# Causal attention: one exponential over all four heads of a step

## What is computed

```python
def _attn(x, ln_w, ln_b, conv_w, attn_w, proj_w, n_head):
    ...
    q = q * cos + _rotate_half(q) * sin
    k = k * cos + _rotate_half(k) * sin
    scores = jnp.einsum('bqhd,bkhd->bhqk', q, k) / jnp.sqrt(jnp.float32(D))
    causal = jnp.tril(jnp.ones((T, T), dtype=bool))
    scores = jnp.where(causal, scores, jnp.float32(-1e+30))
    p = jax.nn.softmax(scores, axis=-1)
    y = jnp.einsum('bhqk,bkhd->bqhd', p, v).reshape(B, T, C)
    return y @ proj_w
```

## Time and profile before

| | |
|---|---|
| median of 3 runs | 433.37 us (432.72 to 433.51) |
| the profiled execution: its own time, its span | 433.3 us, 431.1 us |
| busy: TensorE matmuls | 384.4 us, 89% |
| busy: VectorE, ScalarE, GpSimd | 296.1 us (69%), 174.7 us (41%), 90.8 us (21%) |
| mean granted TensorE clock | 0.967 |
| the 64 exponentials (L983) | 42.6 us busy, from 150.9 to 223.3 us |
| the 32 steps | 149.6 to 223.3 us |

### The profile page before, as it was taken

One profiled execution on the slowest core, in us unless ns is written; L12 is line 12 of the kernel. 1 busy time (PEld: TensorE's weight loads), 2 busy tenths in 40 slices (PEclk: granted clock), 3 DMA queues, 4 the chain that ended last, 5 costly groups with the idle time before them and its releaser, 6 DMA issues.

```text
span 431.1 us, 6269 instructions
## 1 busy us (share of the span) xinstructions
PE 384.4 (89%) x2440; PEld 255.2 (59%) x2440; DVE 296.1 (69%) x662; ACT 174.7 (41%) x257; POOL 90.8 (21%) x87
## 2 busy tenths in 40 slices
PE   2888998998899499989989999999897899998856
PEld 0445777864555245444444666666475788877745
DVE  5678889485998857634324433344589999999766
ACT  1144442655232045566662222222324244444674
POOL 9004445000501300001000000000025344444500
PEclk9999998999999659999999999999999999999996
DMA  5460000037873000035000000000000000000001
GB/s 160 145 151 0 0 2 0 2 104 220 263 204 100 9 0 2 2 119 185 1 2 0 2 0 2 0 1 2 0 2 0 2 0 2 0 2 0 2 2 49
DMA packets 14864, 18.69 MB, mean 43 GB/s; under 512 B 2485, under 2 KB 11885, under 8 KB 14829
## 3 DMA queue, kind: packets, MB, share of 16 engines
q1 hardware_dynamic: 13634, 17.25, 13.6%
q10 hardware_dynamic: 1200, 1.05, 0.7%
HBM read 12.84 MB, written 5.34 MB: 42 GB/s over the span
## 4 chain that ended last, share of the span: by engine, by line
PE 65%; DVE 25%; issue 4%; ACT 2%; DMA 2%; POOL 1%; SPq 1%; POOLq 0%; DVEq 0%
PE PS L1037 60%; DVE mB L687 4%; DVE usum L534 4%; PE PS L1095 3%; DVE mraw L526 3%; DVE big L543 3%; DMA big<-in_A_WkT 1%; DVE big L858 1%; DVE XN L512 1%; ACT big L983 1%; PE PS L1046 1%; DVE stats L501 1%; DVE nm L671 1%; PE PS L1284 1%; DVE umax L530 1%
## 5 line engine op out<-in xcount | busy, mean ns | idle before, releaser
L1037 PE MATMUL PS<-big 128*128 128x128 f32 (+10 forms) x686 | 121.5, 304 | 13.8 <-DVE mB L687 7.2
L1037 PEld LDWEIGHTS PS<-big 128*128 128x128 f32 (+4 forms) x686 | 78.7, 162 | 55.6 <-ACT big L983 15.0
L888 ACT ACTIVATE big<-PS 128x1280 f32<-128x1280 f32 (+4 forms) x36 | 35.6, 998 | 86.7 <-PE PS L1095 70.3
L438 POOL TENSOR_TENSOR big<-big,urec 128x1024 f32<-128x1024 f32 x24 | 45.6, 1899 | 102.2 <-DVE urec L536 102.2
L687 DVE TENSOR_REDUCE mB<-PS 128x2 f32<-128x256 f32 (+5 forms) x86 | 51.1, 648 | 14.6 <-PE PS L1037 13.9
L983 ACT ACTIVATE big<-PS 128x1024 f32<-128x1024 f32 (+3 forms) x64 | 42.6, 703 | 40.2 <-PE PS L1037 40.0
L1037 PE MATMUL PS<-XT,big 128*128 128x512 f32 x128 | 57.2, 595 | 0.0
L1037 PE MATMUL PS<-cstb 128*128 128x128 bf16 x256 | 51.6, 230 | 0.0
L526 DVE TENSOR_REDUCE mraw<-PS 128x3 f32<-128x462 f32 (+1 forms) x72 | 40.1, 582 | 13.8 <-PE PS L1037 12.0
L762 DVE TENSOR_TENSOR big<-big,PS 128x512 f32<-128x512 f32 x32 | 21.8, 686 | 40.1 <-ACT big L992 39.7
L426 POOL TENSOR_TENSOR rstd<-ve,minus_half 128x4 f32<-128x4 f32 (+2 forms) x13 | 13.0, 1006 | 169.5 <-DVE ve L507 169.4
(11 more groups left out here) (142 smaller groups left out, 456.5 us busy)
## 6 DMA issues: line engine op xcount, KB each, us to landing
scr_qk<-big SPq DMA_DIRECT2D x12, 384.0 KB, 3.6
big<-scr_qk SPq DMA_DIRECT2D x16, 288.0 KB
big<-in_wv SPq DMA_DIRECT2D x1, 2048.0 KB, 8.3
X<-in_x ACTq DMA_DIRECT2D x2, 256.0 KB, 3.5
big<-in_A_WoT ACTq DMA_DIRECT2D x1, 512.0 KB, 5.7
cw<-in_C_Wk SPq DMA_DIRECT2D x1, 512.0 KB, 3.8
cw<-in_C_Wv SPq DMA_DIRECT2D x1, 512.0 KB, 4.7
cw<-in_C_WqT SPq DMA_DIRECT2D x1, 512.0 KB, 6.6
```

The costliest lines, as they stand in the source:

```text
L438: pool.tensor_tensor(pn[:, 0:GH * P].rearrange("p (h k) -> p h k", h=GH), Pt[u % 3][:, :, 0:KM], r.to_broadcast([P, GH, KM]), ALU.mult).th ...
L888: return act.activation(dst, src, ACT.Copy, scale=scale)
L1037: return pe.matmul(o, lhsT, rhs, start=start, stop=stop)
```

## The change

ScalarE's loop runs over the 32 steps. One exponential reads banks 0 to 3 at once, 4 x w elements a partition, and writes the step's four slots. It waits for the second `st_mm` of its step, and raises `st_exp` once a step. TensorE's two waits follow: `outputs(s)` waits for `st_exp` of s + 1, and both pairs of step s wait for the one exponential of step s - 1. TensorE's and VectorE's instructions and their order stay. The ring of slots, its depth and the two instructions at steps 17 and 21 stay.

```diff
-            for n in range(B * 4 * QT * 2):
-                s, pair = divmod(n, 2)
+            for s in range(B * 4 * QT):
                 w = T - P * (s % QT)
-                act.wait_ge(st_mm, n + 1)
+                act.wait_ge(st_mm, 2 * s + 2)
                 if s >= 2:
                     act.wait_ge(av_step, s - 1)
-                slot = 4 * (s % 2) + 2 * pair
-                act.activation(PTb[:, slot:slot + 2, 0:w], PS[:, 2 * pair:2 * pair + 2, 0:w], ACT.Exp,
+                slot = 4 * (s % 2)
+                act.activation(PTb[:, slot:slot + 4, 0:w], PS[:, 0:4, 0:w], ACT.Exp,
                                scale=float(HDB) ** -0.5).then_inc(st_exp, 1)
-                if n == 2 * S_TAIL + 1:
+                if s == S_TAIL:
                     turn_outputs(0)
-                if n == 2 * S_LN + 1:
+                if s == S_LN:
                     ln_out("m", XT, *ln2, seqs=(0,))
...
-                pe.wait_ge(st_exp, 2 * s + 2)
+                pe.wait_ge(st_exp, s + 1)
...
                     if s >= 1:
-                        pe.wait_ge(st_exp, 2 * (s - 1) + pair + 1)
+                        pe.wait_ge(st_exp, s)
```

## The result

The changed kernel takes 447.35 us (445.92 to 448.36, 4 runs) against 433.44 us (432.72 to 433.52, 4 runs): a ratio of 1.032, interval 1.029 to 1.036. It is slower, by 13.9 us in the medians. The profiled execution is the quickest of the four: 445.92 us, span 444.1. Against the profiled one of before, 433.3 us with a span of 431.1, that is 12.6 us more, 13.0 in the span.

The account below looks back on a forecast made before the run. TensorE's path was taken as the bound (65% of the span), so added waits cost their full length: 8.6 + 3.4 - 0.5 = 11.5 us on 433.3 gives 444.8 us; own range 442.5 to 447, with the clock's nearer cases to 450.5.

Parts of the forecast that it names:

- the upper bound of 2.04: Exponential of 2048 elements in a wide step: at most two of the old instructions, 2 x 1.02 = 2.04 us.
- The sum over steps 12 to 31: Added waits of TensorE for the one exponential, priced by width over steps 12 to 31: 8.6 us more.
- The covered steps: Steps 16, 18 and 22: transposes, or the projection and the logits, cover the exponential, so no time is added.
- Steps 0 to 11: Only steps 0, 4 and 8, of width 512, lose time, the other nine priced at zero: 3.4 us more.
- the credit: Step 0's wait pushes matmul time past the clock's rise at 160 us, where it takes half: 0.5 us less.
- Cover behind the loop: Last products, copy and experts follow on the same chain, so nothing there gives the added time back: none.
- the clock rival: Pauses in the wide steps also lower TensorE's granted clock: 5 to 6 us more, around 450 us; chance 20%.
- the ring alone: In the loop, scores, exponential and next scores run in turn, with no added clock loss: 444.8 us, chance 77%.
- the clock falls too: Half speed once in each of four or five wide steps: 5 to 6 us more, around 450; chance 20%.
- The price of one fall: One low stretch of TensorE's clock, about 3.2 us at half speed, costs 1.2 us.
- Not slower: In the loop, TensorE's own work covers the exponential and fewer instructions save 0.6 us: 432.7 us; chance 3%.

Follow-up runs that it names:

- both waits: The kernel before with 64 exponentials kept, only both pairs' scores wait for both exponentials of the step before: 436.87 us, ratio 1.007.

## Why the prediction held, and where not

*The sign, the place and the mechanism* were right: the wait moved onto TensorE's path, step by step. Forecast for the four widths 3.25, 2.61, 1.97 and 1.33 us; measured 3.25, 2.60, 1.97 and 1.33. The exponential of 2048 elements: 1.87 forecast, from the line through a three-bank copy, and 1.88 measured; the upper bound of 2.04 was not needed.

*The sum over steps 12 to 31*: 8.6 forecast, 8.45 measured without the fall of the clock (9.40 - 0.95). The covered steps were covered: 16, 18 and 22 take 4.36, 2.56 and 2.96 us, as before. Step 15 lost 0.17 (0.20 forecast).

*Steps 0 to 11*: 3.4 less the credit of 0.5, 2.9 forecast, 2.92 measured. The three wide steps lost 1.17, 1.13 and 1.12 us. The rise of the clock stayed at 160 us, and step 2 took 2.88 us where it took 3.34, which is the credit, 0.46.

*Cover behind the loop*: none, as said. The one change there is 0.70 us, and it is a cost. The same pause of 2.26 us before the second cross-attention's scores stands in both kernels. Before:

```profile
325.22 2.34 PE L1037 MATMUL PS<-kkC,XT 128*128 128x462 f32 x6 [2.26 <-DVE big L543]
```

After:

```profile
337.52 4.03 PE L1036 MATMUL PS<-kkC,XT 128*128 128x462 f32 x6 [2.26 <-DVE big L543]
```

These six matmuls take 2.34 us in the kernel before and 4.03 us after, where the clock fell within 0.2 us of their start. Of these 1.69 us TensorE's later waits take up one: the changed kernel is 12.30 us behind the other where these matmuls start (337.52 - 325.22) and 12.99 at the later scores of this kind that start at 395.90 and 408.89. Which of these pauses is hit changes from kernel to kernel; that later parts may meet a fall once more or once less was said, at 1.2 us, and it came at 0.7.

*The size that was off is the clock's.* 444.8 was the forecast, 445.92 the profiled run, 447.35 the median. Take 0.95 us in the loop and 0.70 behind it from the profiled 445.92, and 444.3 is left. That is 0.5 below the forecast: 0.15 is the sum's, and 0.4 is time around the span, 2.2 us before and 1.8 after.

The forecast's own range ended at 447, so the median lies outside it, by 0.35; only the range widened by the clock rival, to 450.5, takes it in. The median lies halfway between the two numbers, 2.55 above 444.8 and 2.65 below the rival's 450. That the forecast's mechanism was right is known from the profiles and not from the median.

The step that failed is the split of the chances: I set "the ring alone", 77%, against "the clock falls too" at four or five wide steps, 20%, as if nothing lay between. What the profiles show lies between: the ring, and one or two falls from step 12 on beside it. The three profiles of kernels that join there without fillers have one, one and two falls, at twelve pauses of 1.61 us. None of the other profiles has one there: exponentials by pairs or by heads, pairs in the wide steps alone, both waits (longest pause 1.12 us), half the exponential (0.76 us), or matmuls in the pauses.

How often an execution without a profile is hit isn't known, and the 1.4 us by which the median lies above the profiled execution are in no trace. The mean granted clock of the four executions doesn't follow their times: 0.961 for the quickest (445.92) and for the slowest (448.36).

The price of one fall was somewhat high: 1.2 forecast, 0.95, 0.97 and 0.95 measured for the single ones in the loop, 1.9 for the longer one. The 1.2 doesn't follow from the prediction's own row either, since half of the matmul time in 3.2 us is 1.6. A low stretch of 3.4 us in the loop cost less than half of its length, because the slower matmuls first fill what was a pause: TensorE was busy for all 3.00 us from 228.5 on, where it waits for 0.55 us within step 25.

The rule of the Trainium skill that was the rival's ("TensorE: Matmul & The Clock Gate", A second HAM failure mode: psum-queue depth-cycling: brief, frequent idling while cycling PSUM banks lets the clock swing between its levels) holds here in kind: with pauses of 1.61 us the clock did swing, and with the pauses filled it didn't. In size the rival's 450 was 4.1 us off the profiled 445.92, where the forecast was 1.1 off; against the median they were equally far. The mean granted clock from step 12 on is 0.97 (0.91 in the kernel that joins only there), so the clock is down for a small part of the time. Another section of the Trainium skill ("Perfetto Trace Analysis", Optimizing Scalar/DVE Operations), that breaking instructions up may help on an engine that isn't saturated but causes bubbles, holds both ways: joining cost 8.5 us from step 12 on, splitting the wide steps further gave 1.4.

*Not slower* (3%) needed 1.97 us of cover behind the wide scores. Only step 16 has it, and there the change cost nothing.

## What to carry to other kernels

Where one engine fills PSUM banks and another empties them, the size of an instruction is also the size of the hand-over: joining two saves its fixed cost on the emptying engine but moves the whole instruction out of the other's shadow. Price such a change step by step as scores + exponential + hand-overs against what the filling engine has to do anyway, with each width by itself; here that gave the four widths to 0.01 us where no other work covers them. And where such a change leaves TensorE in pauses of half a step, count a fall of its clock now and then as part of the likely case, not as another case.

## What the runs showed of the hardware

- An exponential over four PSUM banks took 1.88 us for 2048 elements, 1.45 for 1536, 1.02 for 1024 and 0.60 for 512, on one line with those over one and two banks: 1024 elements took 1.02 us over two banks and over four, 512 took 0.60 over one, two and four. So crossing banks costs nothing that these rows show.
- More instructions cost a ScalarE that runs back to back little: six in 3.47 us, four with the same elements in 3.46; two of 1024 elements in 1.94, one of 2048 in 1.88. The prediction's upper bound, 2 x 1.02 = 2.04, left out that back-to-back exponentials overlap in the trace.
- The clock could fall at a pause of 1.61 us with TensorE busy for 1.63 of 3.24 us around it, and did so behind some wide steps and not behind others of the same length. Six f32 matmuls in the pause, 1.4 us, kept it at 1.00. Why one wide step is hit and the next is not, no run here shows.
- It can stay down for more than one step: 6.6 us and more with TensorE busy for 6.27 of 6.60, and from 144 to 160 us, over the maxima's scores ahead of the loop and steps 0 to 2.
- A matmul of 128 columns in f32 is two instructions and took 0.23 us back to back.
